# Two attention layers and a chunk attention: shared-bank products moved to the other rounds, copies between the exponentials, one division a batch on GpSimd, and a chunk tree on GpSimd

## The chip, the cores and the metric

One core of one Trainium2 chip. The metric is the device time of the program in microseconds (us), median of the runs. Engines are named as in the profile: PE (TensorE), DVE (VectorE), ACT (ScalarE), POOL (GpSimd), SP (SyncE, which here only issues DMAs). L387 is line 387 of the kernel before.

## What is computed

A model of four layers over x of 16 x 256 tokens of width 128. What matters here:

```python
# layers 0 and 1: 16 heads of 8, RoPE on q and k; layer 0 is causal
scores = einsum('bhqd,bhkd->bhqk', q, k) * SCALE (+ mask)
out = einsum('bhqk,bhkd->bhqd', softmax(scores), v)     # then @ Wo
...
# layer 2: every query meets each chunk of 32 keys by itself
local = softmax(Q K^T of the own chunk) @ V
cross_scores = einsum('bnqe,bmke->bnmqk', Q, K) * scale
cross = einsum('bnmqk,bnke->bnqe', softmax(cross_scores), V)   # V of the query's own chunk
out = (local + cross) @ Wo
```

A router, 32 experts, a slot mixture of experts and an iterated attention follow; the change leaves them alone.

## The kernel before

**attention8** (L251 to L711) runs layers 0 and 1 as 32 batches of 256 tokens, b = 0 to 15 of layer 0 and 16 to 31 of layer 1. A batch has 16 heads, worked in 8 **rounds** j = 0 to 7 of one pair of heads each; p = 8b + j. Every engine has its own program, written as a loop over p, and the engines meet only at semaphores. The order of the work is therefore written out by hand, and a step that waits holds up all that stands behind it on its engine.

In round p PE does, in this order: the scores by key of pair p (`scores_by_key`, L387), the scores of the pair 13 rounds ahead (`scores`, L369), in layer 0 the two masks (L403, L396), one product through **bank M**, and on even j `weigh` (L417, the probabilities of two pairs times v), on odd j `turn_back` (L424, transposes of the sums). Bank M (PSUM bank 7) is shared by all small products, one each round:

| j | before, on PE | the rest of the even or odd round |
|---|---|---|
| 0, 2 | project q, project k of batch b + 3 (L310, L311) | weigh |
| 1 | transpose of the norm between the layers (L242) | turn_back |
| 3 | transpose of the maxima (L349) | turn_back |
| 4 | project v of b + 1 (L320) | weigh |
| 5 | transpose of the output of b - 1 (L332) | turn_back |
| 6 | output projection of b - 1 (L338) | weigh |

The scores by key live in three banks and the scores ahead in three more, so `scores_by_key(p)` waits for the first exponential of pair p - 1, and `scores(ahead)` for the first maximum of the pair before:

```python
            if p:
                pe.wait_ge(*exped(2 * p - 2))
...
            if p >= AHEAD:
                pe.wait_ge(*maxed(2 * p - 2))
```

ACT takes the two exponentials of a pair (L572), copies the sums (L590, odd rounds), and before the exponentials whatever leaves bank M: L248, L578 with two DMA issues of its own (L584), L596. DVE takes the maxima of the pair ahead (L506, two), the rotation of q and k after them (`rope_turn`, L481, L483), v (L494, L496), and each even round `settle`: a reciprocal (L516) and a product (L518) straight from PSUM, which free the bank for the next `weigh`.

The queries and keys of a batch make a long way before they are used: `rope_turn` on DVE, `part` on POOL (L626, L628, L629: sum, high part, low part), two spills by SP (L682), four loads by SP that spread them over the partitions (L702, after both k spills), `lay` on POOL (L639), and only then `scores`. On POOL one batch's order is lay q, lay k, part q, part_maxima (L646, L647), part k. `project(b + 3)` is laid in batch b + 1, before round j = 3 (p + 13 is its first pair).

**chunk_attention** (L1189 to L1379) runs layer 2 in B + 6 = 22 rounds r, a batch of 256 tokens each. E is the table of 256 x 8 chunks x 32 exponentials, 128 x 512 on the chip. DVE: maximum and subtraction from PSUM (L1347, L1348), the sums (L1339), reciprocal (L1340) and the product with the constant own1 (L1341), one round of x (L1328), v (L1319, every other round), and a step of the router (`dve_step`, `cap_dve_step`, L1424 to L1482). POOL scales E (L1368), DVE sums it over the 8 chunks (L1334), POOL spreads the result over a block matrix (L1362), PE transposes it (L1243), and so on to the output. The stage ends at a meeting of all engines.

## Time and profile before

| | us |
|---|---|
| median of 3 runs | 3156.12 (3154.32 to 3156.18) |
| the profiled execution | 3151.76, its span 3150.4 |
| rounds of layers 0 and 1 | 71.75 to 611.7 of the span |
| chunk attention with the router | 697 to 792 |

Busy shares over the whole span: PE 92%, DVE 78%, ACT 70%, POOL 66%. More than half of it, from 1609 us on, is the iterated attention, which isn't touched. So the shares say nothing of this change; the two stages have to be read by themselves. In a timeline row the first number is the start, the second the length; of a merged row (x4) the length is from the first start to the last end. The starts of what follows on the same engine tell what a step costs it.

### The profile page before, as it was taken

The numbers are of one execution on the slowest core, as the hardware profiler recorded it, in microseconds if no ns is written. First come the engines' busy times: TensorE is split into PE (matmuls) and PEld (weight loads), VectorE is DVE, ScalarE is ACT, GpSimd is POOL, SyncE is SP. The second block draws the span as 40 slices with busy tenths as digits, with TensorE's granted clock in tenths as the row PEclk, the third lists the DMA queues.
The fourth block names the chain that finished last, engine by engine and source line by source line (L and its number), as shares of the span: only waits on it lengthen the run. The fifth ranks groups of instructions, "written<-read, shape, count | busy, mean of one in ns | idle before, by whom it ended". The sixth has DMA issues, their size and how long they took to land.

```text
span 3150.4 us, 72205 instructions
## 1 busy us (share of the span) xinstructions
PE 2902.7 (92%) x24663; PEld 2219.1 (70%) x24663; DVE 2461.1 (78%) x5647; ACT 2206.3 (70%) x6156; POOL 2065.3 (66%) x2297
## 2 busy tenths in 40 slices
PE   6999988896999979999979999999999999999997
PEld 4666555564788867887857777777777777777775
DVE  7788899569777764564578888888888888888887
ACT  4666666643455566455358888888888888888886
POOL 2633344223555555335059999999999999999996
PEclk8999999988999989999989999999999999999999
DMA  3222422000000011102000000000000000000000
GB/s 118 74 79 75 143 88 88 22 8 1 1 1 1 1 51 45 44 1 65 1 14 2 1 2 2 1 2 2 2 2 2 1 2 2 2 2 2 2 2 28
DMA packets 68936, 77.16 MB, mean 24 GB/s; under 512 B 8080, under 2 KB 60384, under 8 KB 68448
## 3 DMA queue, kind: packets, MB, share of 16 engines
q1 hardware_dynamic: 64976, 71.10, 7.4%
q8 instruction: 202, 3.31, 0.4%
q10 hardware_dynamic: 3600, 1.46, 0.2%
q14 instruction: 158, 1.29, 0.1%
HBM read 52.61 MB, written 18.87 MB: 23 GB/s over the span
## 4 chain that ended last, share of the span: by engine, by line


## 5 line engine op out<-in xcount | busy, mean ns | idle before, releaser
L3065 POOL TENSOR_TENSOR attn_p<-attn_p,sb_few 128x512 f32<-128x512 f32 x768 | 796.9, 1053 | 108.4 <-DVE sb_few L2840 106.8
L2677 ACT ACTIVATE attn_p<-psum,sb_few 128x256 f32<-128x256 f32 x1536 | 721.5, 480 | 63.9 <-DVE sb_few L2833 63.9
L2833 DVE TENSOR_REDUCE sb_few<-psum 128x2 f32<-128x512 f32 x768 | 509.4, 678 | 13.0 <-PE psum L2531 9.2
L2549 PE MATMUL psum<-sb_kept,attn_p 128*128 128x128 f32 x3072 | 414.2, 278 | 37.2 <-DVE attn_pt L2846 30.5
L2549 PEld LDWEIGHTS psum<-sb_kept,attn_p 128*128 128x128 f32 x3072 | 333.0, 141 | 96.5 <-issue 38.0
L506 DVE TENSOR_REDUCE sb_a_nm<-psum 128x2 f32<-128x512 f32 x512 | 328.6, 684 | 63.0 <-PE psum L396 44.8
L2567 PE MATMUL psum<-attn_pt,attn_v 128*64 128x256 f32 x3072 | 374.1, 385 | 0.2 <-DVE attn_pt L2846 0.2
L572 ACT ACTIVATE sb_a_pt<-psum 128x512 f32<-128x512 f32 x512 | 278.9, 598 | 91.5 <-PE psum L403 63.4
L2677 ACT ACTIVATION_READ_ACCUMULATOR attn_p<-psum,sb_few 128x1 f32 x1536 | 319.4, 208 | 0.0
L2846 DVE COPY attn_pt<-psum 128x512 f32<-128x512 f32 x384 | 263.5, 686 | 32.3 <-PE psum L2549 27.2
L2567 PEld LDWEIGHTS psum<-attn_pt,attn_v 128*64 128x64 f32 x3072 | 201.1, 136 | 117.8 <-issue 32.4
L2685 ACT COPY attn_pt<-psum 128x512 f32<-128x512 f32 x384 | 224.1, 584 | 64.7 <-PE psum L2549 58.5
L2531 PE MATMUL psum<-attn_kh,attn_qh 64*128 64x256 f32 x1536 | 244.7, 315 | 24.2 <-DVE attn_ql L2852 18.4
L1564 POOL TENSOR_TENSOR experts_hh_low<-experts_h,experts_hh_high 128x512 fp32r<-128x512 f32 x136 | 176.0, 1294 | 133.1 <-ACT experts_hh_high L1589 133.1
L2852 DVE TENSOR_TENSOR attn_ql<-psum,attn_qh 128x256 fp32r<-128x256 f32 x384 | 147.2, 418 | 107.2 <-ACT attn_qh L2698 105.6
L2531 PE MATMUL psum<-attn_kl,attn_qh 64*128 64x256 f32 x1536 | 217.9, 280 | 0.0
L2531 PE MATMUL psum<-attn_kh,attn_ql 64*128 64x256 f32 x1536 | 217.5, 279 | 0.0
L2531 PEld LDWEIGHTS psum<-attn_kh,attn_qh 64*128 64x128 f32 x1536 | 145.8, 186 | 95.5 <-DVE attn_ql L2852 68.1
L1584 ACT ACTIVATE experts_sg<-psum 128x512 f32<-128x512 f32 x136 | 81.4, 598 | 153.6 <-PE psum L1645 144.5
L3060 POOL TENSOR_TENSOR attn_qf<-attn_qf 128x512 f32<-128x512 f32 x128 | 171.4, 1339 | 0.0
L2840 DVE RECIPROCAL sb_few<-sb_few 128x2 f32<-128x2 f32 x768 | 114.8, 156 | 63.4 <-ACT attn_p L2677 63.2
L2698 ACT CAST attn_qh<-psum 128x512 fp32r<-128x512 f32 x192 | 113.2, 589 | 63.6 <-PE psum L2567 63.6
(447 smaller groups left out, 7699.2 us busy)
## 6 DMA issues: line engine op xcount, KB each, us to landing
sb_a_spread<-a_spilled SPq DMA_DIRECT2D x64, 256.0 KB, 3.0
a_spilled<-sb_a_part_hi SPq DMA_DIRECT2D x64, 128.0 KB
a_spilled<-sb_a_part_lo SPq DMA_DIRECT2D x64, 128.0 KB
sb_a_spread<-a_spilled SPq DMA_DIRECT2D x64, 128.0 KB, 3.5
sb_gate_up<-in_L_ffn_Wg SPq DMA_DIRECT2D x32, 128.0 KB
sb_gate_up<-in_L_ffn_Wu SPq DMA_DIRECT2D x32, 128.0 KB
sb_down_w<-in_L_ffn_Wd SPq DMA_DIRECT2D x32, 128.0 KB, 2.5
sb_x<-in_L_attn_x SPq DMA_DIRECT2D x4, 512.0 KB, 7.5
```

The costliest lines, as they stand in the source:

```text
L506: dve.tensor_reduce(nm[:, b % 2, at:at + TB], S(p, e).rearrange("p (t n) -> p t n", t=TB), AX.X, ALU.max, negate=True).then_inc(maxed.sem, 1)
L572: act.activation(PTs[p % 4][:, e, :, :], ST(p, e).rearrange("p (k n) -> p k n", k=TB), ACT.Exp).then_inc(exped.sem, 1)
L1564: pool.tensor_tensor(hh_low[i % 3][:, :], hh[i % 3][:, :], hh_high[i % 3][:, :].bitcast(F32), ALU.subtract).then_inc(parted.sem, 1)
L2531: mm = pe.matmul(S(p, e)[:, t * N:(t + 1) * N], a_[n][half(e), hp, t * P:(t + 1) * P], b_[u % 2][half(e), hp, :], start=(n_ == 0), stop=(n ...
L2549: mm = pe.transpose(PT(e)[:, kt * N + t * P:kt * N + (t + 1) * P], Pr[p % 3][:, e, t, kt * P:(kt + 1) * P], c.ident)
L2567: mm = pe.matmul(O(p)[half(e), :], V[u % 2][:, kt, h * HD3:(h + 1) * HD3], PTs[p % 2][:, e, kt, :], start=(kt == 0), stop=(kt == TB - 1))
L2677: ins = act.activation(Pr[p % 3][:, e, t, :], S(p, e)[:, t * N:(t + 1) * N], ACT.Exp, bias=nm[:, p % 4, e, t:t + 1], accum_out=rsum[:, p % ...
L2685: act.copy(PTs[p % 2][:, 0, :, :], PT(0).rearrange("p (k n) -> p k n", k=TB)).then_inc(even.sem, 1)
L2833: dve.tensor_reduce(nm[:, p % 4, e, :], S(p, e).rearrange("p (t n) -> p t n", t=TB), AX.X, ALU.max, negate=True).then_inc(maxed.sem, 1)
L2846: dve.tensor_copy(PTs[p % 2][:, 1, :, :], PT(1).rearrange("p (k n) -> p k n", k=TB)).then_inc(odd.sem, 1)
L3060: pool.tensor_tensor(then, now, then, ALU.subtract).then_inc(differed.sem, 1)
L3065: pool.tensor_tensor(P3, P3, spread(rinv[:, p % 4, e, :], N), ALU.mult).then_inc(normed[e].sem, 1)
```

## The change

In attention8:

- the wide products through bank M go to the odd rounds and the small ones to the even rounds (project q and k at j = 1, 3, the norm's transpose 2, maxima 4, v 5, output transpose 6, output projection 7), and `turn_back` moves ahead of the bank-M product of its round;
- DVE's `settle` goes. ACT copies the 2 x 4 x 9 values from PSUM into a new tile `raw` (`copy_back`, ahead of the exponentials of each even round); once a batch, at j = 3, DVE inverts 128 x 32 sums (`invert_sums`) and POOL divides 128 x 256 values (`divide`, after part k);
- ACT's copies out of bank M and its maxima DMAs go between the two exponentials of a pair;
- DVE rotates q and k at j = 2, 4 ahead of the maxima of that round, lays v at 6, adds at 0; ternary steps of the later weights one round later.

In chunk_attention:

- DVE's product with own1 and its sum over the chunks go; POOL does the product, then the sum as a tree of three additions in place, each waiting for the one before;
- the exponential comes in the same round as its scores, and turn, mix and output two rounds sooner: B + 4 = 20 rounds.

```diff
@@ attention8, pe_program, the loop over p
+            if p % 2 and 3 <= p < NP + 3:
+                turn_back((p - 3) // 2)
-            if j in (0, 2) and -1 <= b and b + 3 < NB8:
+            if j in (1, 3) and -1 <= b and b + 3 < NB8:
                 project(b + 3, j // 2)
-            elif j == 1 and 3 <= b < B + 3:
+            elif j == 2 and 3 <= b < B + 3:
                 pe.wait_ge(*turned_q(2 * (b + 3)))
                 between.turn(b - 3, M)
...
-            elif j == 3 and -1 <= b and b + 1 < NB8:
+            elif j == 4 and -1 <= b and b + 1 < NB8:
                 turn_maxima(b + 1)
-            elif j == 4 and 0 <= b and b + 1 < NB8:
+            elif j == 5 and 0 <= b and b + 1 < NB8:
                 project_v(b + 1)
-            elif j == 5 and b >= 1:
+            elif j == 6 and b >= 1:
                 turn_out(b - 1)
-            elif j == 6 and b >= 1:
+            elif j == 7 and b >= 1:
                 through_wo(b - 1)
             if p % 2 == 0 and 2 <= p < NP + 2:
                 weigh((p - 2) // 2)
-            if p % 2 and 3 <= p < NP + 3:
-                turn_back((p - 3) // 2)
@@ dve_program
-        def settle(i):
...
-            c.dve_own(dve.reciprocal(rinv[:, :, :], src[:, :, :, HD8]))
...
+        def invert_sums(b):
+            dve.wait_ge(*settled((b + 1) * PB // 2 - 1))
+            if b:
+                dve.wait_ge(*divided(b - 1))
+            dve.reciprocal(rinv[:, :, :], raw[b % 2][:, :, :, HD8]).then_inc(sums_inverted.sem, 1)
...
-            if p % 2 == 0 and 4 <= p < NP + 4:
-                settle((p - 4) // 2)
-            if j == 7 and b >= 1:
-                add(b - 1)
+            if j == 3 and b >= 1:
+                invert_sums(b - 1)
+            if j == 0 and b >= 2:
+                add(b - 2)
+            elif j in (2, 4) and -1 <= b and b + 3 < NB8:
+                rope_turn(b + 3, j // 2 - 1)
+            elif j == 6 and 0 <= b and b + 1 < NB8:
+                lay_v(b + 1, 0)
+                lay_v(b + 1, 1)
             if ahead < NP:
                 maxima(ahead, 0)
                 maxima(ahead, 1)
@@ act_program
+        def copy_back(i):
+            b, j = divmod(i, PB // 2)
+            act.wait_ge(*backed(i))
+            if b >= 2 and j == 0:
+                act.wait_ge(*divided(b - 2))
+            src = OT.rearrange("p (t r c) -> p t r c", t=TB, c=ROW)[:, :, :, 0:HD8 + 1]
+            act.copy(raw[b % 2][:, :, 4 * j:4 * j + 4, :], src).then_inc(settled.sem, 1)
...
-            if j == 6 and b >= 1:
-                copy_out(b - 1)
+            if p % 2 == 0 and 4 <= p < NP + 4:
+                copy_back((p - 4) // 2)
             if p % 2 and 3 <= p < NP + 3:
                 copy_sums((p - 3) // 2)
+            if 2 <= b < B + 2 and j == 4:
+                between.root(b - 2)
+            if 0 <= p < NP:
+                exps(p, 0)
             if j == 2 and 3 <= b < B + 3:
                 between.move(b - 3, M)
-            if 2 <= b < B + 2 and j == 4:
-                between.root(b - 2)
-            if j == 4 and -1 <= b and b + 1 < NB8:
+            elif j == 4 and -1 <= b and b + 1 < NB8:
                 lay_maxima(b + 1)
+            elif j == 6 and b >= 1:
+                copy_out(b - 1)
             if 0 <= p < NP:
-                exps(p, 0)
                 exps(p, 1)
             if 2 <= b < B + 2 and j == 7:
                 between.normalise(b - 2)
@@ pool_program
+        def divide(b):
+            pool.wait_ge(*sums_inverted(b))
+            if b >= 2:
+                pool.wait_ge(*out_turned(b - 2))
...
             if b + 1 < NB8:
                 part(b + 1, 1)
+            if b >= 3:
+                divide(b - 3)
@@ chunk_attention, pool_program
-                    pool.wait_ge(*summed(b))
...
+            for b in range(B):
+                own, e = c.pool_own, E[b % R].rearrange("p (t m) k -> p t m k", m=NK)
+                pool.wait_ge(*zed(b))
+                own(pool.tensor_tensor(zi[:, b % R, :], zi[:, b % R, :], own1, ALU.mult))
+                own(pool.tensor_tensor(E[b % R][:, :, :], E[b % R][:, :, :], spread(zi[:, b % R, :], CK), ALU.mult))
+                m = NK // 2
+                while m:
+                    own(pool.tensor_tensor(e[:, :, 0:m, :], e[:, :, 0:m, :], e[:, :, m:2 * m, :], ALU.add))
+                    m //= 2
```

The order of PE in rounds j = 2 and 3 of a batch of layer 0, before (a_q, a_k: queries and keys; a_pt: exponentials; a_w: weights of the projections):

```order
L387 MATMUL psum<-sb_a_q,sb_a_k 128x256 x4
L369 MATMUL psum<-sb_a_k,sb_a_q 128x256 x4
L403 MATMUL psum<-sb_mask,sb_future 128x128 x4
L396 MATMUL psum<-sb_future,sb_mask 128x128 x4
L310 MATMUL psum<-sb_xnT,sb_a_w 128x256
L311 MATMUL psum<-sb_xnT,sb_a_wr 128x256
L417 MATMUL psum<-sb_a_pt,sb_a_v 32x256 x8
```

and in the round after it, j = 3, with the change (L391, L373, L407, L400 are the four score and mask products):

```order
L391 MATMUL psum<-sb_a_q,sb_a_k 128x256 x4
L373 MATMUL psum<-sb_a_k,sb_a_q 128x256 x4
L407 MATMUL psum<-sb_mask,sb_future 128x128 x4
L400 MATMUL psum<-sb_future,sb_mask 128x128 x4
L428 MATMUL psum<-sb_kept,sb_a_sums 128x128 x2
L314 MATMUL psum<-sb_xnT,sb_a_w 128x256
L315 MATMUL psum<-sb_xnT,sb_a_wr 128x256
```

The projection has left the round of `weigh` (L417) and stands behind `turn_back` (L428).

ACT at j = 4, before (the exponentials of round 3, then what leaves bank M, then those of round 4):

```order
L572 ACTIVATE sb_a_pt<-psum 128x512 x2
L209 ACTIVATE between_rstd<-between_var 128x2
L210 ACTIVATE between_rstd<-between_rstd 128x2
L578 COPY sb_a_nm_rows<-psum 64x128
L584 DMA sb_a_q<-sb_a_nm_rows 4x8x128 x2
L572 ACTIVATE sb_a_pt<-psum 128x512 x2
L590 COPY sb_a_sums<-psum 128x256
```

and with the change:

```order
L596 COPY sb_a_raw<-psum 128x2x36
L210 ACTIVATE between_rstd<-between_var 128x2
L211 ACTIVATE between_rstd<-between_rstd 128x2
L570 ACTIVATE sb_a_pt<-psum 128x512
L576 COPY sb_a_nm_rows<-psum 64x128
L582 DMA sb_a_q<-sb_a_nm_rows 4x8x128 x2
L570 ACTIVATE sb_a_pt<-psum 128x512
L588 COPY sb_a_sums<-psum 128x256
```

The two DMA issues have gone between the exponentials, with the copy of the sums (L588) behind them. POOL in one batch of the chunk attention, with the change (before: L1368 and L1362 alone):

```order
L1373 TENSOR_TENSOR chunks_zi<-chunks_zi,sb_table 128x16
L1374 TENSOR_TENSOR chunks_e<-chunks_e,chunks_zi 128x512
L1377 TENSOR_TENSOR chunks_e<-chunks_e 128x2x128
L1377 TENSOR_TENSOR chunks_e<-chunks_e 128x2x64
L1377 TENSOR_TENSOR chunks_e<-chunks_e 128x2x32
L1381 TENSOR_TENSOR chunks_wb<-chunks_e,sb_table 128x256
```

## Rows read from the trace of the kernel before

**Rows 1.** Windows (us; busy PE, PEld, DVE, ACT, POOL; PEclk): layer 0, layer 1, chunks.

```profile
109.06:327.20 218.14, 212.15 (x2650) 146.50 (x2651) 181.26 (x481) 140.48 (x322) 91.43 (x137) 1.00 0.24 76
377.63:566.19 188.56, 167.84 (x1868) 98.58 (x1868) 173.86 (x396) 127.15 (x273) 75.97 (x123) 0.99 0.29 89
697.00:792.00 95.00, 65.58 (x319) 49.02 (x318) 86.99 (x233) 31.93 (x65) 26.57 (x32) 0.83 0.00 1
```

**Rows 2.** Timeline of PE, rounds j = 2 and 3 of batch 9 of layer 0.

```profile
240.98 0.50 PE L387 MATMUL psum<-sb_a_q,sb_a_k 32*128 32x256 f32 x4
241.30 0.50 PE L369 MATMUL psum<-sb_a_k,sb_a_q 32*128 32x256 f32 x4
241.74 0.40 PE L403 MATMUL psum<-sb_mask,sb_future 128*128 128x128 bf16 x4
242.19 0.65 PE L310 MATMUL psum<-sb_xnT,sb_a_w 128*128 128x256 f32 x2
243.21 1.07 PE L417 MATMUL psum<-sb_a_pt,sb_a_v 128*32 128x256 f32 x16
244.21 0.38 PE L387 MATMUL psum<-sb_a_q,sb_a_k 32*128 32x256 f32 x2
244.65 0.40 PE L403 MATMUL psum<-sb_mask,sb_future 128*128 128x128 bf16 x4
245.49 0.38 PE L424 MATMUL psum<-sb_kept,sb_a_sums 128*128 128x128 f32 x2
245.79 0.50 PE L387 MATMUL psum<-sb_a_q,sb_a_k 32*128 32x256 f32 x4
```

**Rows 3.** Timeline of ACT beside and after it (ACTq: its DMA issues).

```profile
244.34 0.37 ACT L590 COPY sb_a_sums<-psum 128x256 f32<-128x256 f32 x1 [1.09 <-PE psum L417]
246.41 0.24 ACT L578 COPY sb_a_nm_rows<-psum 64x128 f32<-64x128 f32 x1
246.68 1.10 ACTq L584 DMA_DIRECT2D sb_a_q<-sb_a_nm_rows  x2
247.88 1.09 ACT L572 ACTIVATE sb_a_pt<-psum 128x512 f32<-128x512 f32 x2 [1.24 <-PE psum L403]
```

**Rows 4.** Timeline of ACT, the norm at the end of round 7.

```profile
236.55 0.87 ACT L229 ACTIVATE between_normed<-sb_x,between_offset,between_rstd 128x128 f32<-128x128 f32 x2
```

**Rows 5.** Timeline of DVE, `settle` and what follows, in layer 1.

```profile
460.16 0.20 DVE L516 RECIPROCAL sb_a_rinv<-psum 128x8 f32<-128x8 f32 x1
460.53 1.28 DVE L506 TENSOR_REDUCE sb_a_nm<-psum 128x2 f32<-128x512 f32 x2
461.73 0.47 DVE L481 SCALAR_TENSOR_TENSOR sb_a_t<-psum,sb_bk,sb_table 128x256 f32<-128x256 f32 x1
```

**Rows 6.** Timeline of POOL, from the keys of one batch to those of the next.

```profile
459.50 1.04 POOL L639 CAST sb_a_k<-sb_a_spread 128x1024 fp32r<-128x1024 f32 x1 [1.19 <-DMA sb_a_spread<-a_spilled]
463.73 0.40 POOL L628 CAST sb_a_part_hi<-sb_a_rot 128x256 fp32r<-128x256 f32 x1
464.21 0.79 POOL L629 TENSOR_TENSOR sb_a_part_lo<-sb_a_rot,sb_a_part_hi 128x256 fp32r<-128x256 f32 x1
474.17 1.04 POOL L639 CAST sb_a_k<-sb_a_spread 128x1024 fp32r<-128x1024 f32 x1 [0.88 <-DMA sb_a_spread<-a_spilled]
```

**Rows 7.** Groups by line and form, DVE and POOL, 697 to 792 us.

```profile
L1334 DVE TENSOR_REDUCE chunks_w<-chunks_e 128x64 f32<-128x512 f32 x16 | 16.3, 1019 | 0.0
L1341 DVE TENSOR_TENSOR chunks_zi<-chunks_zi,sb_table 128x16 f32<-128x16 f32 x16 | 2.8, 174 | 0.6
L1368 POOL TENSOR_TENSOR chunks_e<-chunks_e,chunks_zi 128x512 f32<-128x512 f32 x16 | 16.8, 1048 | 24.6 <-DVE chunks_zi L1341 24.6
L1362 POOL TENSOR_TENSOR chunks_wb<-chunks_w,sb_table 128x256 f32<-128x256 f32 x16 | 9.8, 613 | 45.6 <-DVE chunks_w L1334 45.6
```

**Rows 8.** The tile chunks_e: shortest, median and longest of a line (ns).

```profile
L1368 POOL TENSOR_TENSOR chunks_e<-chunks_e,chunks_zi x16: 1047/1048/1050, 706.5 to 782.2; 128x512 f32<-128x512 f32 x16
```

**Rows 9.** Groups by line and form: POOL's smallest elementwise form of two inputs.

```profile
L647 POOL TENSOR_TENSOR sb_a_nm_parts<-sb_a_nm,sb_a_nm_parts 128x32 fp32r<-128x32 f32 x10 | 2.5, 252 | 0.8
```

136 lines of the change are left out of this document (58 added, 78 removed).

## The prediction

> **What bounds the kernel now.** The shares of the whole span are those of the iterated attention, so I read windows first [rows 1]. Twelve batches of layer 0 take 218.14 us, 18.18 each, and PE is busy 212 of them: PE looks like the bound. Twelve batches of layer 1 take 188.56, 15.71 each, with DVE busy 92% and PE 89%. In the chunk attention DVE is busy 87.0 of 95.0 us, PE 65.6, POOL 26.6: there DVE is the bound.
>
> Then the timeline of PE [rows 2], since a busy PE can be a badly fed one. The even round j = 2 lasts from 240.98 to 244.21 = 3.23, the odd one to 245.79 = 1.58. In the long round L369 starts 0.32 after L387 because it waits for DVE's first maximum; in the short one, right behind `weigh`, both start together, and the masks follow 0.44 later (244.21 to 244.65). So short rounds end in a wait for DVE or ACT that the next round pays, and long rounds are PE's work alone. The unevenness is what costs: `weigh` takes 1.00 (243.21 to 244.21), a projection 1.02 (242.19 to 243.21), and both stand in even rounds.
>
> Third, ACT [rows 3, 4]: the maxima of a batch cost it 0.24 for the copy and 1.10 for two DMA issues; the next exponential starts only at 247.88. The norm costs 0.87 at the end of round 7. Fourth, DVE's `settle` [rows 5]: 460.16 to 460.53 = 0.37 each, four a batch. Last, the way of the keys [rows 6]: POOL lays one batch's at 459.50 and the next's at 474.17, 14.67 later, with POOL at work in between only until 465.00; 9.2 us of it are spills, loads and their waits.
>
> A difference of 0.2% (6 us) is about what a measurement of this kernel can tell from none.
>
> **Layer 0, batch by batch.** PE's own work with the change: scores side by side 0.44 and masks 0.45 (241.74 to 242.19) are 0.9 in 8 rounds = 7.2; four `weigh` 4.0; four `turn_back` at 0.30 (245.49 to 245.79) 1.2; two projections 2.04; v and the output projection, each half a projection's columns, 0.51 by that and 0.6 as I take it, 1.2; three small transposes about 0.2 each 0.6 [rows 2]. Sum 16.2. Behind 0.8 us or more of other PE work the first maximum (half of 1.28 [rows 5]) and the first exponential (half of 1.09 [rows 3]) are ready in every round, so the 0.32 goes. What is late next are two things on ACT.
>
> - Round 4: the first exponential ends 1.4 into the round, then copy 0.24, issues 1.10, second exponential 0.6, copy of the sums 0.37: 3.8. PE's round 4 is 2.1 long and wants the sums 0.9 into the next, at 3.0. `turn_back`, v and the rest wait 0.8.
> - Round 7: two exponentials end at 2.0, the norm at 2.85, and only then comes `copy_back`, on which `weigh` of round 0 waits. PE is there at 1.8 + 0.9 = 2.7, ACT at 3.1: 0.4.
>
> Rotations ahead of the maxima add perhaps 0.1. So 16.2 + 1.3 = 17.5 against 18.18: 0.7 saved in some 13 batches, 9; half of that in batches 14 and 15, 0.7. The opening pays about 1.5, since the queries and keys of batch 2 are projected one round later each and the first maxima wait for them. Layer 0: **-8**.
>
> **Layer 1.** By engine loads a batch could fall to 13.4 to 14.5: without masks PE has 16.2 - 8 x 0.45 = 12.6 and ACT, with 127.15 / 12 = 10.6 [rows 1], issues 1.1 and new copies 1.0, about 12.7, and they wait for each other as above. DVE loses 4 x 0.37 = 1.5 and gains one inversion. But the keys' way does not shorten. Laid keys, part q, part_maxima, part k, spills and loads follow one another on POOL and SP in 14.67 when nothing else is late [rows 6], and `scores` at j = 3 cannot start before they are laid. With the projection of k now at j = 3, one round later, rotation 0.9 (two passes of 0.47 [rows 5]), part k about 2.0 (0.79, 0.40 and 0.79 [rows 6]), 9.2 + 1.0 to the laid keys and 1.5 from scores to the next projection, the loop through PE is 14.7 as well. Loads that land late cost a few tenths: 14.9 to 15.0. That is 0.8 less than 15.71, in 13 batches 10.4. The last three batches have no such loop, 0.5 more; the end adds inversion, division and copy in a row where `settle` was, 0.9. Layer 1: **-10**.
>
> **New small work.** `copy_back` moves 2 x 36 columns from PSUM on ACT. Its cost lies between 0 and the 0.37 of 256 columns; I take 0.24, that of the 128-column copy, the nearest in size [both rows 3], four a batch, hidden except in round 0 as above; at 0.37 it costs 0.13 more there, 4 us in all. The inversion of 32 values costs between the 0.20 of one reciprocal of 8 and four times that [rows 5], ahead of DVE's maxima at j = 3, hidden. The division is 128 x 256 on POOL: between 0.61 [rows 7] and 0.79 [rows 6]. It stands behind part k and ahead of the next `lay`, which waits over 7 us for its load; `turn_out` needs it only at j = 6. All hidden; without that cover each would cost its 0.8, 25 us in all.
>
> **Chunk attention.** DVE loses L1334, 16.3, and L1341, 2.8 [rows 7]: 19.1, less 0.08 for each of 32 instructions, since the next one starts before they end (L506 ends at 461.81, L481 starts at 461.73 [rows 5]): 16.5; two own waits fewer a batch give 0.5 or more. It stays the bound at about 78 us if POOL keeps up. POOL's batch: product of 128 x 16 (at most 0.25 [rows 9]), E 1.05, tree of 256, 128 and 64 additions: the first 0.79 as L629 [rows 6], the others 0.48 and 0.33 on a straight line from there to the 0.25 of 32 columns, block 0.61 [rows 7]; 3.5, with five own waits of 0.08 (the gap between L628 and L629 [rows 6]) 3.9. Sixteen are 62, inside 75. A late POOL would hold ACT's copy of the transposes and so the next exponential; it decides only above some 4.5 a batch. PE and ACT are idle for a third and more. I take **-17**.
>
> The Trainium skill speaks against this last part: "GPSIMD Engine Reference", section "Engine selection", gives elementwise work with two inputs to VectorE, with GPSIMD about two times slower, and section "Key points" warns of contention with DVE instructions that have two SBUF inputs. The row speaks against the contention here: L1368 took 1047 to 1050 ns in all 16 batches, beside a DVE that was almost always busy [rows 8]. By the rule the tree would cost more than I take, and the third stage would gain nothing; this is the third rival.
>
> **Sum.** -8 - 10 - 17 = -35. The profiled execution had 3151.76, so it would have 3117; its time lies 4.4 under the median of the runs, and a median of 3156.12 becomes 3121.
>
> **The rivals.**
>
> 1. The waits on ACT don't appear, because round lengths adapt, and loads land sooner: layer 0 at PE's 16.2, layer 1 at 14.3. Then 13 x 2.0 + 13 x 1.4 + 17 = 61: 3095. For it: the regular rounds of PE. Against it: the 14.67. Chance 0.2.
> 2. The first two layers gain nothing: ACT's issues, norm and copies lengthen the rounds as much as the balance shortens them (1.3 of stalls against 2.0, twice that is enough). Only the third stage gains: 3139. Chance 0.17.
> 3. The tree is as slow as the rule has it. At 5.4 us a batch POOL needs 86 + 9 = 95 us and the stage is as before: 3156 - 18 = 3138. Chance 0.08.
> 4. Slower: ACT becomes the engine that sets every round. In layer 0 it is busy 140.48 / 12 = 11.7 a batch [rows 1]; with issues 1.1 and new copies 1.0 that is 13.8. If the second exponential, now behind a bank-M copy that waits for PE, and `copy_back`, which waits for `turn_back`, tie PE and ACT in both directions, each batch grows. It decides from 0.55 a batch (32 x 0.55 = 17, the gain of the third stage). At 0.8: 3156 + 26 - 17 = 3165. For it: three new cross waits in each pair of rounds. Against it: ACT is busy only 64 to 67% now [rows 1]. Chance 0.06.
> 5. The parts cancel within 0.2%: 3156. Chance 0.04. My forecast keeps 0.45.
>
> Faster by over 0.2%: 0.45 + 0.2 + 0.17 + 0.08 = 0.90; within: 0.04; slower: 0.06. The range reaches to rival 1 below and past rivals 2 and 3 above: 3093 to 3145.
>
> **What would show it.** Steps right: even and odd rounds of layer 0 within 0.5 us of each other at 2.0 to 2.3; batches of 17.5; in layer 1 batches of 15.0 with PE waiting for POOL's L639 at j = 3; in the third stage POOL's six instructions within 3.9, DVE still over 85% busy, the stage at 78. Wrong: a layer 1 at 14.3 or below (the loop isn't one), a copy of the sums that is not late in round 5, a tree above 4.5 us, or E's product no longer 1.05. A time over 3150 would mean that ACT ties the rounds.

## The result, and the profile after

| | before | changed |
|---|---|---|
| median of the runs, us | 3156.15 (3154.32 to 3159.07, 4 runs) | 3139.27 (3137.17 to 3141.61, 4 runs) |
| ratio | | 0.9947, 95% interval 0.9935 to 0.996 |
| time and span of the profiled run | 3151.76 and 3150.4 | 3140.26 and 3138.9 |

17 us faster: the sign and the range were right, the size was half of the 35 forecast. The stages below are the distances between their first PE instructions, read from the trace. The changed kernel was run and profiled a second time later on (`e15_again`), and that row says how far one profile can be trusted.

| stage, us | before | changed | changed again | forecast |
|---|---|---|---|---|
| up to the first `scores_by_key` | 71.75 | 74.48 | 70.39 | +1.5 |
| layer 0 (batches 0 to 15) | 290.14 | 283.75 | 280.86 | -9.5 |
| layer 1 (to the next layer's first PE instruction) | 249.79 | 246.96 | 251.15 | -10 |
| the layer after it (same code) | 81.27 | 82.03 | 82.82 | 0 |
| chunk attention | 99.04 | 88.14 | 86.55 | -17 |
| the rest (same code) | 2358.4 | 2363.6 | 2364.3 | 0 |

Layer 0 came as forecast or nearly, layer 1 gained nothing that two profiles agree on, and the chunk attention gained 11 to 12.5 of 17. The "rest" of before's profile is 5 to 6 us shorter than the changed kernel's, with identical code. Its profiled run also lay 4.4 us under the median of before, and the two may have one cause, so I count stages against stages and totals against medians. The table counts the chunk attention from its first PE instruction, before at 692.96; the window of [rows 1] and the forecast's 78 begin at 697. In the table's measure the forecast of this stage is 82.

Windows of the changed kernel (us; busy PE, PEld, DVE, ACT, POOL; PEclk), nine steady batches of layer 0, seven of layer 1, and the chunk attention, beside [rows 1]:

```profile
168.40:324.30 155.90, 151.50 (x1991) 102.12 (x1990) 126.83 (x298) 111.28 (x281) 67.26 (x108) 1.00 0.26 78
438.20:543.00 104.80, 91.39 (x1088) 55.05 (x1086) 92.47 (x176) 77.64 (x183) 48.16 (x77) 1.00 0.28 91
687.03:775.17 88.14, 66.90 (x323) 49.05 (x324) 69.98 (x201) 32.69 (x67) 58.51 (x96) 0.86 0.03 7
```

Layer 0 is 17.3 us a batch (155.90 / 9) where it was 18.18, layer 1 14.97 (104.80 / 7) where it was 15.71. In the whole chunk attention DVE fell from 88% busy (86.99 of 99.04) to 79%, where over 85% was forecast, and POOL rose from 27% to 66%: no engine is full any more.

The timeline of PE, end of round 1 to start of round 3 of batch 9 of layer 0, beside [rows 2]:

```profile
240.86 0.39 PE L428 MATMUL psum<-sb_kept,sb_a_sums 128*128 128x128 f32 x2
241.09 0.60 PE L314 MATMUL psum<-sb_xnT,sb_a_w 128*128 128x256 f32 x2
242.05 0.39 PE L391 MATMUL psum<-sb_a_q,sb_a_k 32*128 32x256 f32 x2
242.06 0.38 PE L373 MATMUL psum<-sb_a_k,sb_a_q 32*128 32x256 f32 x2
242.49 0.40 PE L407 MATMUL psum<-sb_mask,sb_future 128*128 128x128 bf16 x4
243.07 0.44 PE L243 MATMUL psum<-sb_kept,between_normed 128*128 128x128 f32 x2
243.44 1.07 PE L421 MATMUL psum<-sb_a_pt,sb_a_v 128*32 128x256 f32 x16
244.44 0.38 PE L391 MATMUL psum<-sb_a_q,sb_a_k 32*128 32x256 f32 x2
```

The projection now stands with `turn_back` (L428), `weigh` (L421) with a small transpose, and L391 and L373 start together in every round: no wait for a maximum is left in layer 0. The eight rounds of a steady batch take 2.22, 2.09, 2.39, 2.09, 2.31, 2.29, 2.22, 1.67 = 17.28.

ACT in round 4 of batch 8, then PE in round 5, beside [rows 3]:

```profile
230.68 0.26 ACT L576 COPY sb_a_nm_rows<-psum 64x128 f32<-64x128 f32 x1
230.97 1.10 ACTq L582 DMA_DIRECT2D sb_a_q<-sb_a_nm_rows  x2
232.12 0.60 ACT L570 ACTIVATE sb_a_pt<-psum 128x512 f32<-128x512 f32 x1 [1.18 <-issue]
232.62 0.37 ACT L588 COPY sb_a_sums<-psum 128x256 f32<-128x256 f32 x1
```

```profile
233.03 0.44 PE L428 MATMUL psum<-sb_kept,sb_a_sums 128*128 128x128 f32 x2 [0.40 <-ACT sb_a_sums L588]
```

The stall that the forecast named is there, with 0.40 us instead of 0.8.

What went wrong in batch 4 (22.37 us where its neighbours take 17.28): DVE, POOL and PE, timelines.

```profile
144.66 1.12 DVE L217 SCALAR_TENSOR_TENSOR between_newton<-between_var,between_rstd 128x2 f32<-128x2 f32 x1
145.81 1.19 DVE L218 TENSOR_TENSOR between_newton<-between_newton,between_rstd 128x2 f32<-128x2 f32 x1
147.04 1.01 DVE L221 SCALAR_TENSOR_TENSOR between_rstd<-between_newton,between_rstd 128x2 f32<-128x2 f32 x1
148.08 0.16 DVE L222 SCALAR_TENSOR_TENSOR between_offset<-between_mv,between_rstd 128x2 f32<-128x2 f32 x1
```

```profile
142.04 2.37 POOL L834 TENSOR_TENSOR sb_x<-sb_x,sb_L_attn_bo 128x1024 f32<-128x1024 f32 x1
144.49 2.50 POOL L994 TENSOR_TENSOR sb_x<-sb_x,opening_xn 128x512 f32<-128x512 f32 x2
146.99 1.04 POOL L648 CAST sb_a_q<-sb_a_spread 128x1024 fp32r<-128x1024 f32 x1
```

```profile
148.90 0.79 PE L373 MATMUL psum<-sb_a_k,sb_a_q 32*128 32x256 f32 x4 [2.16 <-DVE sb_a_nm L510]
```

Three DVE instructions on two values a partition take 1.0 to 1.2 us. Each ends within 0.05 us of a POOL instruction that began before it: L217 at 145.78, where the first of the two L994 (1.27 each) ends, at 145.76; L218 at 147.00, the second at 146.99; L221 at 148.05, L648 at 148.03. With POOL idle L222 takes 0.16. DVE's maxima come late, PE waits 2.16 us, and the windows show what followed in this run:

```profile
128.00:146.00 18.00, 16.96 (x222) 11.39 (x221) 15.08 (x34) 12.42 (x32) 11.47 (x16) 1.00 0.25 76
146.00:169.00 23.00, 20.40 (x230) 13.73 (x231) 17.07 (x38) 13.11 (x34) 8.47 (x13) 0.85 0.19 61
```

The granted clock fell to a mean of 0.85; at the lower of its two levels (1.2 GHz) L373 takes 0.79 for four, at the upper 0.50. The Trainium skill, "SBUF — State Buffer", section "Who interferes with whom", describes the first half of this: a DVE instruction with two SBUF inputs and a GpSimd instruction that reads SBUF take the same read interface, and whichever was issued first keeps the other out until it has finished. The trace agrees to 0.05 us, and the third of the POOL instructions has one input only. The fall of the clock doesn't always follow. Nine profiles have this order of work: in seven batch 4 takes 19.56 to 19.73 at a clock of 1.00, in one 21.23 at 0.92, here 22.37.

The way of the keys in layer 1, POOL's timeline, beside [rows 6]:

```profile
457.10 1.04 POOL L648 CAST sb_a_k<-sb_a_spread 128x1024 fp32r<-128x1024 f32 x1 [1.25 <-DMA sb_a_spread<-a_spilled]
462.95 0.62 POOL L664 TENSOR_TENSOR sb_a_o<-sb_a_raw,sb_a_rinv 128x256 f32<-128x256 f32 x1
471.88 1.05 POOL L648 CAST sb_a_k<-sb_a_spread 128x1024 fp32r<-128x1024 f32 x1 [1.32 <-DMA sb_a_spread<-a_spilled]
```

14.78 from keys to keys; the division (L664) hides ahead of the load, as forecast.

What the first three batches of layer 1 pay, PE's timeline in batches 17 (first two rows) and 18, and DVE's ahead of the third row:

```profile
375.75 1.07 PE L421 MATMUL psum<-sb_a_pt,sb_a_v 128*32 128x256 f32 x16 [0.66 <-ACT sb_a_raw L596]
379.58 0.44 PE L243 MATMUL psum<-sb_kept,between_normed 128*128 128x128 f32 x2 [0.53 <-DVE sb_a_t L487]
400.74 0.27 PE L353 MATMUL psum<-sb_kept,sb_a_nm_parts 128*64 128x128 f32 x1 [1.23 <-DVE sb_a_t L487]
```

```profile
399.00 0.68 DVE L1017 TENSOR_REDUCE opening_amax<-sb_shared 128x1 f32<-128x512 f32 x1
```

In round 0 `weigh` waits for `copy_back`, which stands behind the norm on ACT. In round 2 the transpose of the norm waits for bank M, which the rotation of q frees. In batch 18 a reduction for the later weights stands on DVE ahead of the rotation of k, so the transpose of the maxima is 1.23 late and the sums after it 0.95.

Groups of POOL in the chunk attention, by form, beside [rows 7]:

```profile
L1374 POOL TENSOR_TENSOR chunks_e<-chunks_e,chunks_zi 128x512 f32<-128x512 f32 x16 | 18.7, 1171 | 1.2
L1377 POOL TENSOR_TENSOR chunks_e<-chunks_e 128x256 f32<-128x256 f32 x16 | 13.4, 840 | 1.3
L1381 POOL TENSOR_TENSOR chunks_wb<-chunks_e,sb_table 128x256 f32<-128x256 f32 x16 | 9.8, 614 | 1.3
L1377 POOL TENSOR_TENSOR chunks_e<-chunks_e 128x128 f32<-128x128 f32 x16 | 7.3, 456 | 1.3
L1377 POOL TENSOR_TENSOR chunks_e<-chunks_e 128x64 f32<-128x64 f32 x16 | 6.0, 373 | 1.3
L1373 POOL TENSOR_TENSOR chunks_zi<-chunks_zi,sb_table 128x16 f32<-128x16 f32 x16 | 3.6, 222 | 19.7 <-DVE chunks_zi L1347 19.5
```

The tile chunks_e, L1374 alone, beside [rows 8]:

```profile
L1374 POOL TENSOR_TENSOR chunks_e<-chunks_e,chunks_zi x16: 1047/1049/2994, 697.9 to 761.6; 128x512 f32<-128x512 f32 x16
```

One of the 16 took 2994 ns. Undisturbed, POOL's batch repeats after 3.73 us (forecast 3.9). Its timeline and DVE's show one that is disturbed, PE's what it does to the clock:

```profile
720.97 2.53 POOL L1377 TENSOR_TENSOR chunks_e<-chunks_e 128x256 f32<-128x256 f32 x3
723.58 0.61 POOL L1381 TENSOR_TENSOR chunks_wb<-chunks_e,sb_table 128x256 f32<-128x256 f32 x1
725.84 1.66 POOL L1377 TENSOR_TENSOR chunks_e<-chunks_e 128x256 f32<-128x256 f32 x3
```

```profile
721.95 1.37 DVE L1450 TENSOR_TENSOR moe_values<-moe_values,moe_z 128x1024 f32<-128x1024 f32 x1
```

```profile
724.25 0.44 PE L1263 MATMUL psum<-sb_kept,chunks_wb 128*128 128x128 f32 x2 [1.73 <-POOL chunks_wb L1381]
724.97 1.72 PE L1254 MATMUL psum<-chunks_k,chunks_q 128*128 128x256 f32 x4
```

The same three additions take 1.66 us alone and 2.53 beside the router's product L1450. PE waits 1.73 us, and its scores then take 1.72 instead of 1.03. One of the three is the long one: it takes 1.18 instead of 0.32, begins 0.37 after L1450 and ends 0.18 after it. Here POOL loses, because DVE was first.

### The profile page after: what moved, and what is told of

Same layout as the page of the kernel before. It is cut to its first block and busy times, and to the rows that moved or that the text cites. A ratio compares the mean times of both kernels' runs of the same rounds, so it can differ in the third digit from the quotient of the medians.

```text
span 3138.9 us, 72141 instructions
## 1 busy us (share of the span) xinstructions
PE 2888.9 (92%) x24662; PEld 2208.2 (70%) x24663; DVE 2418.7 (77%) x5391; ACT 2226.1 (71%) x6284; POOL 2118.3 (67%) x2393
## 5 line engine op out<-in xcount | busy, mean ns | idle before, releaser
L570 ACT ACTIVATE sb_a_pt<-psum 128x512 f32<-128x512 f32 x512 | 287.7, 600 | 129.4 <-PE psum L407 64.7
L2860 DVE COPY attn_pt<-psum 128x512 f32<-128x512 f32 x384 | 263.8, 687 | 32.0 <-PE psum L2563 26.3
```

The costliest lines, as they stand in the source:

```text
L570: act.activation(PTs[p % 4][:, e, :, :], ST(p, e).rearrange("p (k n) -> p k n", k=TB), ACT.Exp).then_inc(exped.sem, 1)
L2860: dve.tensor_copy(PTs[p % 2][:, 1, :, :], PT(1).rearrange("p (k n) -> p k n", k=TB)).then_inc(odd.sem, 1)
```

## Experiments

All start from the changed kernel unless said otherwise, and each is timed against before on the same chip; ratios are to before. The stage lengths quoted are read as in the table above. Where a stage's code was the changed one, the profiles have layer 0 at 280.7 to 281.3 (283.75 in the first, 282.2 in `e13_layer1_back`), layer 1 at 246.8 to 253.1 in nine profiles with a median of 250.8, the chunk attention at 86.3 to 88.2. So against before's 249.79 (250.10 in `e2_third`) layer 1 gained nothing.

**The kernel again, and each half alone.**

> The changed kernel itself, beside the two others on the same chip. Theory: ratio to before 0.9935 to 0.996 as found, median within 3 us of 3139. It also tells how far one kernel's runs lie apart (before's lay between 3151.5 and 3165).

3140.31 us (3137.36 to 3145.01), ratio 0.9951 (0.9937 to 0.9965). Batch 4 took 19.73, at a clock of 1.00, instead of 22.37 at 0.85; batch 18 took 18.07, at 0.91, instead of 16.81 at 1.00. The gain is firm; one profile's stage isn't, to some 4 us.

`e1_layers`: `chunk_attention` of before in the changed kernel. `e2_third`: the changed `chunk_attention` in before.

> Only the first two layers are changed; the chunk attention is that of before. Theory (the stages add up, each saves what its own stretch of the two traces shows: 6.7 us in the two layers, 10.9 in the chunk attention): 3156 - 7 = 3149, within 3 us, with the opening and batch 4 as long as in the changed kernel (batch 4 at 22.4 us). Rival (the chunk attention's gain is partly one of a later stage or of the state it starts in): a time over 3153 or under 3145.

> Only the chunk attention is changed; the first two layers are those of before. Theory: 3156 - 11 = 3145, within 3 us, stage of 88 us, and layer 0 with batches of 18.2 and no batch above 20. Rival (the gain of the third stage is larger alone, because the layers of the change leave it something behind): under 3141.

`e2_third` 3147.32, ratio 0.9969 (0.9956 to 0.9981), the stage 88.17: some 8 to 10 us of the whole are the chunk attention's, near the 11 expected. `e1_layers` 3153.57, ratio 0.9992 (0.9983 to 1.0001): a miss. The two layers and the start are 8.3 shorter in its profile, yet the layer after them is 1.6 longer, the chunk attention 1.2 and the rest, 2365.9, 7.5 longer than before's. Windows before and here, the 54 us from 346 us after the start of the experts on:

```profile
1138.00:1192.00 54.00, 49.71 (x337) 46.95 (x338) 34.96 (x73) 37.34 (x126) 30.59 (x27) 0.97 0.01 1
```

```profile
1132.62:1186.62 54.00, 49.05 (x320) 45.95 (x319) 32.27 (x68) 36.65 (x118) 30.07 (x27) 0.92 0.00 1
```

The same code at a lower granted clock. Seventeen profiles other than before's have a rest of 2358.4 (`e9_router_early`) to 2365.9, so before's 2358.4 is at the short end. `e2_third`, with before's first layers, has 2363.6, so the changed layers aren't the cause of the longer rest. What sets it was not tried; it stays open why the layers alone show 1.6 us and the halves (1.6 + 7.8) don't add up to 17.

**POOL beside DVE.** `e3_finish_waits`:

```diff
             if 2 <= b <= beside.NN + 1:
+                if b >= 4:
+                    pool.wait_ge(*between.refined(b - 4))
                 beside.finish(b - 2)
```

> POOL's additions that finish the opening (lines 834 and 994) wait in two batches until DVE has refined the norm. Theory (DVE's small two-input instructions took about 1.1 us each instead of 0.16 because POOL's additions ran beside them; DVE's delay made PE wait, and the clock fell): L217, L218 and L221 are back at 0.16 to 0.2 in batches 2 and 3, batch 4 takes 17.3 us instead of 22.4, its granted clock stays at 1.00, and the time is 4 to 6 us less: 3133 to 3135. Rival (the clock would have fallen anyway, or the additions now wait where something else needs them): L217 to L221 short, but batch 4 still over 20 us and the time 3139, or a new wait for the additions.

3134.85, ratio 0.9932 (0.992 to 0.9945). The tile between_newton (shortest, median, longest, ns), and the window of batch 4:

```profile
L217 DVE SCALAR_TENSOR_TENSOR between_newton<-between_var,between_rstd x16: 148/151/152, 123.5 to 381.0; 128x2 f32<-128x2 f32 x16
L218 DVE TENSOR_TENSOR between_newton<-between_newton,between_rstd x16: 160/160/161, 123.7 to 381.2; 128x2 f32<-128x2 f32 x16
```

```profile
146.00:169.00 23.00, 22.32 (x285) 15.23 (x283) 19.31 (x47) 16.28 (x40) 12.63 (x20) 1.00 0.20 60
```

In the changed kernel the longest were 1118 and 1195. Batch 3 is back from 18.14 to 17.71, batch 4 from 22.37 to 17.70, layer 0 from 281 (283.75) to 278.35. Three more kernels with this wait have batch 4 at 17.70 to 17.72 too. The contention is shown, and so is that the clock, where it fell, fell behind it. The price is 2.5 us (against `e15_again`) where the clock stays, as in most profiles, and up to 5.4 where it falls. The 0.4 above 17.28 that stay in each of the two batches were not looked into.

**The place of the copies.** `e4_copies_ahead` puts the three copies of bank M ahead of `exps(p, 0)`.

> The three copies of the shared bank (L240's move, lay_maxima with its two DMA issues, copy_out) stand on ACT ahead of a pair's two exponentials again, not between them; all else as changed. Theory (a copy waits for PE's step of the same round, so ahead of the exponentials it holds up both, and the DMA issues delay the first as well): rounds 2, 4 and 6 of layer 0 grow by 0.5 to 1 us, the batch to 18.3 or more, the whole by 20 us or more: 3160. Rival (the place is indifferent, since ACT has slack in these rounds, and the gain of layer 0 comes from the other rounds alone): within 5 us of 3139.

3169.04, ratio 1.004 (1.0028 to 1.0053): 30 us more than the changed kernel, and slower than before. Batches 18.40 as expected, round 4 3.57 instead of 2.31, and layer 1 loses as well (263.8). PE in it, nine batches of layer 0:

```profile
L391 PE MATMUL psum<-sb_a_q,sb_a_k 32*128 32x256 f32 x290 | 36.4, 328 | 10.7 <-ACT sb_a_pt L570 10.7
```

10.7 / 9 = 1.2 us a batch of waiting for the exponential that stands behind the copy and the DMA issues. With PE's product and ACT's copy in the same round the copy is better between the exponentials.

**The division and the rounds apart.** `e5_divide_dve` has DVE divide behind its inversion. `e11_rounds_back` has before's rounds and orders in both layers, with the changed copy back, inversion and division.

> The division of a batch (L664, 0.63 us on POOL) is done by DVE, right behind the inversion; all else as changed. Theory (layer 1's batch is set by the way of the keys through POOL and SP, and layer 0's by PE and ACT, so 0.4 to 0.6 us more on DVE a batch hides in both): batches 5 to 12 stay at 17.28, batches 21 to 23 and 26, 27 at 14.65 to 14.9. The additions of the opening start 0.63 earlier and still meet part of DVE's refinement, so batch 4 takes 18 to 21 instead of 22.4. Time 3136 to 3139. Rival (layer 1 is set by DVE): these batches 0.4 to 0.6 longer, the time 3143 or more.

> The first two layers have the rounds and the order of before (shared bank's products in even rounds of PE with weigh, copies ahead of the exponentials but one round after PE's step, rotations in their old places); only the copy back on ACT, the inversion once a batch and the division on POOL are kept of the change, and the chunk attention is as changed. Theory (layer 0's 0.9 a batch comes from the balance of the rounds alone, since DVE waits in it anyway; in layer 1 DVE, then at 92%, loses some 1.2 us a batch and the loop of the keys takes over at 14.7 to 15.2): batches 5 to 12 at 18.0 to 18.4, batches 21 to 27 at 14.7 to 15.2; 3139 + 11 = 3150. Rival (the division in DVE's path delays the rotations in layer 0 too, as 0.43 a batch when DVE divides once a batch suggests): batches 5 to 12 at 17.4 to 17.8, and 3144.

`e5_divide_dve`: 3149.46, ratio 0.9971 (0.996 to 0.9983), slower than the changed kernel by 6 to 10 us, by ratios or by medians: the rival's time. Inversion and division are short (0.35 and 0.43),

```profile
L522 DVE TENSOR_TENSOR sb_a_o<-sb_a_raw,sb_a_rinv 128x256 f32<-128x256 f32 x9 | 3.9, 431 | 0.3
```

but the batch is 0.43 longer in layer 0 too (17.71), all in round 4 (2.75 instead of 2.31). They stand ahead of the maxima and the rotation of k, which PE's round 4 needs; that this is the way was read from the order, not tried. Batch 4 is at 18.69, as expected. A DVE that is busy 81% of the time (126.83 of 155.90) is no cover for what stands ahead of a step that is waited for.

`e11_rounds_back`: 3140.12, ratio 0.9951 (0.9937 to 0.9965), 10 us less than expected and equal to the changed kernel. Layer 0 292.2: batches of 18.29, so all of its gain comes from the new rounds and orders together. Layer 1 243.4, batches 21 to 27 at 15.10 to 15.12 without exception: in this profile the division off DVE gives 6.4 us with the old rounds, and none with the new ones. The rest, 2360.3, is 3 to 4 us shorter than the changed kernel's, so a part of the 10 is not the layers'.

| us | layer 0 | layer 1 |
|---|---|---|
| before | 290.1 | 249.8 |
| new division, old rounds | 292.2 | 243.4 |
| new division, new rounds | 280.9 | 251.2 |
| the same, first profile | 283.8 | 247.0 |

Where in layer 1: batches 16 to 18 take 16.34, 16.24, 16.81 in the changed kernel and 15.68, 15.79, 15.39 with old rounds. The waits shown above stretch rounds 0 and 2 there (2.17 to 2.27 and 2.41, against 1.45 each later), and round 4 of batch 18 takes 2.94 instead of 2.33 in all ten profiles that have the new rounds up to it. Behind it the clock falls in six of the ten: batch 18 takes 16.8 in four, 18.07 in one and 19.25 to 19.35 in five, where before has 15.90. Other batches run to 17 us in single profiles (20 in two). In `e6_k_early` the later part of batch 18 has a mean clock of 0.72:

```profile
395.00:407.00 12.00, 9.82 (x90) 5.95 (x89) 8.42 (x17) 6.36 (x16) 4.17 (x6) 0.72 0.33 100
```

**The loop of the keys.** `e6_k_early`:

```diff
+    early = lambda b: B + 4 <= b < NB8 - 3
...
-            if j in (1, 3) and -1 <= b and b + 3 < NB8:
-                project(b + 3, j // 2)
+            if j in ((1, 2) if early(b) else (1, 3)) and -1 <= b and b + 3 < NB8:
+                project(b + 3, 0 if j == 1 else 1)
```

> In batches 20 to 28 the keys of batch b + 3 are projected at j = 2 instead of j = 3 and rotated at j = 3 instead of j = 4; all else as changed. Theory (the loop of the keys, 14.65 and more in the steady batches, runs through the projection at j = 3): the loop shortens by about one round, and batches 21 to 27 fall to 13.2 to 14.0, where DVE, with about 13.2 us of work a batch, is the next bound; 3139 - 8 = 3131, with 3129 to 3133 as what it may be. Rival (something else sets 14.7, as the loads, which start when POOL has parted the keys but wait in SP's order behind the queries' way): batches at 14.6 or more and a time of 3139 or more.

3139.07, ratio 0.994 (0.9923 to 0.9957), batches of 15.12: the rival's numbers, but not for its reason. The wait for the keys is gone (round 3 1.19 instead of 1.95 to 2.8), so the loop was real. But round 2 became 3.10: `weigh` and a projection together again, behind a wait for the bank,

```profile
441.55 0.70 PE L315 MATMUL psum<-sb_xnT,sb_L_attn_Wk 128*128 128x256 f32 x2 [0.52 <-DVE sb_a_t L488]
```

Batch 21 of the changed kernel is 1.45 + 1.80 + 1.45 + 1.95 + 2.33 + 2.27 + 2.02 + 1.38 = 14.65. With round 3 at the 1.80 of round 1, whose work is the same, it would be 14.5, and batches 20 to 27 have a mean of 15.02: the loop costs 0.5, between 0.15 and 1.0. Behind this bound lies the next one, close by.

**The second layer with the old rounds.** `e13_layer1_back` switches PE, DVE and ACT to before's order at b = 16 (`old = lambda b: b >= B`); `e14_with_wait` adds the edit of `e3_finish_waits`.

> From batch 16 on (the second layer) PE, DVE and ACT follow the order of the rounds of before (shared bank's products in even rounds, copies ahead of the exponentials); the first layer keeps the changed order, and the copy back, inversion and division stay as changed everywhere. Theory (in the second layer the balanced rounds lose: batches 16 to 18 took 16.2 to 16.8 instead of 15.4 to 15.8 with the old rounds, and PE's waits for the keys at j = 3 bring low-clock rounds; old rounds gave a steady 15.11): batches 19 to 27 at 15.1, the second layer 3 to 4 us shorter than in the changed kernel, batch 4 as slow as there; 3 to 5 us less than the changed kernel run beside it. Rival (the second layer's gain belongs to the lay of the first, or is lost at the switch): within 1.5 us of it.

> The same, with the opening's additions held until DVE's refinement in two batches as well. Theory: both gains add, batch 4 at 17.7; 7 to 10 us less than the changed kernel run beside it, and faster than both kernels. Rival (the clock takes one of them back elsewhere): 5 us less or under.

3134.56, ratio 0.9931 (0.9917 to 0.9945), and 3133.31, ratio 0.9922 (0.991 to 0.9935), beside 3140.31 of the changed kernel: 5.8 and 7.0 us less. `e14_with_wait` has the lowest median found; its interval lies just clear of that of the changed kernel beside it, but overlaps those of nine other variants. In its profile layer 0 takes 278.75, layer 1 245.74, with batches of 15.23. The first gain is a little more than expected, the two together at the lower edge, and the 1.3 us between them are within the noise. The four profiles with old rounds and the new division have layer 1 at 243.4, 248.1, 245.7 and 251.5 (`e11_rounds_back`, `e13_layer1_back`, `e14_with_wait`, `e16_all`), where the new rounds have a median of 250.8: some 4 us less in the median, with single batches of 16 to 18 us in two of them.

**The chunk attention.** `e7_own_dve` moves L1373 to DVE; `e8_one_input` replaces two of the router's two-input passes on DVE by reductions, and so leaves out the centring and the division of the router's scores:

```diff
-            dve.tensor_tensor(sc[:, :, :], sc[:, :, :], spread(self.m[:, :], NE2), ALU.subtract).then_inc(self.centred.sem, 1)
+            dve.tensor_reduce(self.z[:, :], sc[:, :, :], AX.X, ALU.max).then_inc(self.centred.sem, 1)
...
-            own(dve.tensor_tensor(sc[:, :, :], sc[:, :, :], spread(self.z[:, :], NE2), ALU.mult))
+            own(dve.tensor_reduce(self.m[:, :], sc[:, :, :], AX.X, ALU.max))
```

> In the chunk attention the product of the inverted sums with own1 (L1373, 0.22 us) is back on DVE: POOL's batch falls from 3.75 to 3.45 us, DVE's grows by about 0.2. Theory (neither engine sets the stage alone; the rounds that are too long are those in which PE waited and the clock fell): the stage stays within 2 us of 88.1. Rival 1 (POOL sets the rounds): 16 x 0.3 = 5 us less. Rival 2 (DVE sets them): 3 us more.

> Two of the router's steps that run on DVE beside the chunk attention, L1444 and L1450 (each with two inputs of 1024 elements in SBUF, 1.22 and 1.37 us), are replaced by reductions of the same 1024 elements, with one input and 1.21 us each: the router's scores are neither centred nor divided by their sum. DVE's load is unchanged. Theory (these two held up POOL's tree, 2.5 us instead of 1.66; PE waited for the weights, the clock fell, and the next projections took 2.9 us instead of 1.9): POOL's three additions take 1.66 in every batch up to the router's last steps, the clock stays higher and the stage falls by 3 to 5 us from 88.1. Rival (POOL's lateness and the clock have another cause): the stage within 1 us of 88.1.

`e7_own_dve`: 3140.19, ratio 0.9946 (0.993 to 0.9962), the stage 91.1, 3 to 5 longer: rival 2. POOL's waits for DVE's inverted sums go from 19.5 us to 25.4, so work on DVE ahead of that hand-over lengthens the stage, though DVE is busy only 79%. (The whole took no longer than the changed kernel, so this is the profile's stage alone.) `e8_one_input`: 3135.2, ratio 0.9931 (0.9916 to 0.9946), the stage 84.6, 1.6 to 3.5 shorter. The 8 us from 18 us after the stage's start on, changed kernel and this one:

```profile
705.03:713.03 8.00, 6.89 (x23) 4.86 (x24) 3.29 (x6) 3.56 (x6) 7.10 (x14) 0.60 0.00 0
```

```profile
706.01:714.01 8.00, 8.00 (x40) 6.33 (x40) 4.71 (x9) 4.72 (x9) 6.51 (x11) 0.83 0.00 0
```

Clock 0.83 instead of 0.60, and PE does 40 matmuls instead of 23. The router's last steps still meet POOL (L1374 took 3003 ns once); what they cost was not tried.

`e9_router_early` runs the router's passes at the start of the stage; `e16_all` is `e14_with_wait` with that and L1373 on DVE from batch 9 on.

> In the chunk attention the router's steps on DVE and ACT that need two passes of 1024 elements (maximum, subtraction, exponential, sum, product) run at the start of the stage, in which DVE is idle for over 6 of the first 10 us and POOL has nothing to do; the choice of the experts and its masks follow in rounds 1 to 9 instead of 7 to 16. Theory (in the changed kernel these passes meet POOL's tree and product, 2.5 to 3.0 us instead of 1.66 and 1.05, PE waits, the clock falls; and the last ones, 2.45 and 2.25 us, lengthen the tail): the stage falls from 88.1 to 80 to 84 us, since DVE's work in it (about 68 us) is as before, the granted clock 18 to 26 us into the stage is over 0.8 instead of 0.57 to 0.60, and the time is 4 to 8 us less: 3132 to 3135. Rival (DVE's sum of work sets the stage, whatever the order): the stage within 1.5 us of 88.

> As the one with both edits, and in the chunk attention the router's passes over 1024 elements at the start of the stage, its choice in rounds 1 to 9, and from batch 9 on the product with own1 on DVE. With the router early alone POOL ran back to back at 3.73 us a batch from batch 9 on while DVE had gaps. Theory (in that half POOL sets the period): the period falls to 3.45 there, the stage from 87.2 to 85 us, and the time is 1 to 3 us under that of the kernel without it. Rival (DVE or PE takes over at once): the stage at 87 or more.

`e9_router_early`: 3135.87 (3129.94 to 3143.39), ratio 0.9938 (0.9922 to 0.9955); the stage 87.2, the rival's number, and the clock 18 to 26 us into it 0.64. The contention wasn't gone but had moved: one addition took 2.87 us instead of 0.73 beside the router's TENSOR_SCALAR of 2.43, which now ran at 733 us. `e16_all`: 3136.56, ratio 0.9932 (0.9918 to 0.9945), 3 us more than without, which is within the noise; the stage is 86.4, between what theory and rival gave, and POOL's period from batch 9 on 3.59, not 3.45. In `e9_router_early` from 739 us on POOL runs without a gap at 3.73 us a batch, while DVE is busy 18.8 of 24:

```profile
735.00:759.00 24.00, 17.24 (x98) 13.34 (x96) 18.77 (x35) 8.73 (x21) 21.65 (x37) 0.93 0.01 1
```

In this half POOL sets the pace. In the other POOL waits for DVE (five waits of 0.15 to 2.3 us), so that DVE's way to the inverted sums does; that one half's saving lands on the other engine is my reading of these runs, not a thing tried.

**The opening, and three edits together.** `e10_opening` projects and rotates batch 2's queries and keys one round earlier; `e12_three` is this with `e3_finish_waits` and `e9_router_early`.

> Queries and keys of batch 2 are projected at j = 0 and 2 and rotated at j = 1 and 3, as early as before the change; all else as changed. Theory (the start of batch 0 came 2.5 us later, 74.28 against 71.75, because these two projections stood one round later each, and the first maxima wait for them): batch 0 starts at 72 to 72.5, and the time is 2 us less, 3137. Rival (the reordered maxima and rotations on DVE or the clock cause it): the start stays at 74.

> The changed kernel with the three edits together: additions of the opening after DVE's refinement in two batches, the opening's projections as early as before, the router's passes at the start of the chunk attention. Theory (they act in stretches that don't overlap): the gains add up, 4.5 + 2 + 4 to 8 us: 3125 to 3129, ratio to before 0.990 to 0.9915, better than both kernels. Rival (what is gained is lost where the clock recovers later, as when only the layers were changed): 3132 or more.

`e10_opening`: 3136.7 (3128.43 to 3142.31), ratio 0.9938 (0.9922 to 0.9955); the first `scores_by_key` at 69.3 (71.4 in `e12_three`, with the same edit), but batch 0 takes 20.15 (20.36), and of the profiles with the changed opening the first starts lie between 70.4 and 74.5. Not settled: too small beside that. `e12_three`: 3133.72 (3123.81 to 3138.78), ratio 0.9926 (0.9909 to 0.9943): the rival, 5 us short of its forecast, with a chunk attention of 89.9.

## Why the prediction was half right

The sum -8 - 10 - 17 failed in two terms: the -10 of layer 1, where the profiles show nothing gained, and 5 of the -17 of the chunk attention. The first layer's term was right in size, in part by luck.

- **Layer 0, "16.2 + 1.3 = 17.5".** Right in size: 17.28. The wait for the sums was 0.40, not 0.8, and PE waited for no `copy_back` in round 0 (forecast 0.4); against that PE is busy 151.5 / 9 = 16.8 a batch, not 16.2. Two errors cancel, so that the sum came within 0.2 is luck. That the new rounds and orders carry the gain is shown by `e11_rounds_back`.
- **Batches 3 and 4.** The forecast had nothing there; it costs 2.5 to 5.4 us. The step that failed: "All hidden" for the division on POOL, with cover looked for on POOL alone. `e3_finish_waits` shows the mechanism. Neither half of the edit does it alone: without the division batch 4 takes 18.7 (`e5_divide_dve`), with it and the old rounds 18.55, 0.26 above its neighbours (`e11_rounds_back`), with both 19.7. In before L216 begins 0.2 ahead of the end of POOL's last addition and takes 0.21, so the two only just touch. That it is the later place of part k on POOL by which the new rounds shift them was not tried.
- **"The row speaks against the contention".** That step failed in its logic. [rows 8] shows POOL's durations in a kernel in which they met none of DVE's long two-input passes: one, for instance, ran at 725.38 to 726.60, and POOL was idle then from 724.89 on. Who came first decides who is long: L217 to L221 are DVE's, L1377 beside L1450 is POOL's. The Trainium skill's warning of contention ("GPSIMD Engine Reference", section "Key points"), which I set aside, was right. Its "two times slower" (section "Engine selection") wasn't borne out as a price: the tree's cost came out as mine. The tree itself was sized well: 0.73, 0.46, 0.32 us where 0.79, 0.48 and 0.33 were forecast.
- **Layer 1, "14.9 to 15.0".** Nearly right for batches 19 to 27 of the first profile, 15.06 in the mean (15.69 before), and the loop was as described: 0.6 saved in nine batches, 5.7 us. Wrong for the layer, and here lies the largest error of the whole sum. "0.8 in 13 batches" counted batches 16 to 28 as alike. Batches 16 to 18 cost 2.2 us more than before in the first profile (16.2 to 16.8 each, against 15.6 to 15.9) and 3.4 in the second. The wait for `copy_back` that I had put at 0.4 in layer 0 stands there, at 0.66, beside two waits for a rotation (0.53 and 1.23) for which I had no term; rounds at the lower clock follow. From batch 28 to the layer's end another 0.7 and 3.1 are lost. With the old rounds the new division gives 6.4 us in one profile and 3 us in the median of four, with the new rounds none.
- **Chunk attention, "the bound at about 78 us if POOL keeps up".** DVE's load came out as forecast (87.0 - 16.5 = 70.5; measured 69.98), the stage didn't: 88.1 where the forecast is 82. Two steps failed. The first is "Sixteen are 62, inside 75": POOL doesn't have the whole stage. Its first product starts 10.7 us after the stage's start and its last 13.8 before its end (687.2, 697.9, 761.6 and 775.4). At the forecast 3.9 a batch fifteen periods are 58.5, and 58.5 + 24.5 = 83. So POOL had no slack at all in a stage of 82, and every wait of it counts. The second is "it decides only above some 4.5 a batch". Measured are 63.6 / 15 = 4.24 a period, where POOL alone takes 3.73. Of the 7.7 us between them 5.2 are waits of POOL for DVE's inverted sums, with the clock at 0.60 in part of it, and 1.8 are two additions made longer by the router's passes (0.73 to 1.66 and 0.32 to 1.18). `e8_one_input` shows that the contention and what hangs on it are 1.6 to 3.5 of the stage, `e7_own_dve` that more waiting for DVE lengthens it.
- **Small terms.** copy_back 0.23 (forecast 0.24), inversion 0.35 (between 0.20 and 0.80), division 0.63, L1373 0.22: all right. The opening's +1.5 can't be told from a spread of 4.1.
- **Rivals.** "The first two layers gain nothing" came closest in time (3139) and is wrong as a mechanism: layer 0 gained 6 to 9 us, layer 1 nothing. Rival 3's 3138 is as near and as wrong: POOL's batch is 3.73, not 5.4. ACT as the bound did not appear in the changed order, and did, at 30 us, where the copies stood ahead.

## What to carry to other kernels

Sum a stage as fill, periods and tail of each engine, since an engine that starts 11 us late has no room for work that fits its share of the whole. Evening out rounds paid where PE's own work sets them (layer 0) and not where other waits sit in the evened places (layer 1): decide it per stage, and count the first and last batches of a stage by themselves. When work moves to POOL, look at DVE's two-input instructions around it as well, however small, and at what waits behind them; and trust a few microseconds of one profile only after a second.
